# Latent attention on one core: probabilities turned by VectorE in 32x32 blocks, a batch's values summed in eight array tiles, exponentials of both heads ahead of the query copy

## What is computed

```python
q = (x @ W_q).reshape(B, S, N_HEADS, D_HEAD).transpose(0, 2, 1, 3)
latent = x @ W_kv_down
kv = (latent @ W_kv_up).reshape(B, S, N_HEADS, D_HEAD).transpose(0, 2, 1, 3)
scores = jnp.einsum('bhqd,bhkd->bhqk', q, kv) * scale
probs = jax.nn.softmax(scores, axis=-1)
out = jnp.einsum('bhqk,bhkd->bhqd', probs, kv)
out = out.transpose(0, 2, 1, 3).reshape(B, S, N_HEADS * D_HEAD)
return out @ W_o
```

## Time and profile before

| | |
|---|---|
| median of 3 runs | 1045.13 us (1040.69 to 1045.65) |
| the profiled execution | 1047.63 us, of which its span is 1045.9 us |
| busy over the span | PE 94%, PE weight load 57%, DVE 66%, ACT 47%, POOL 27% |
| this stage in the trace | first matmul at 707.65 us, last ACT copy ends at 873.01 us: 165.36 us |
| its parts | 32 pairs to 844.48, then the 64 mix matmuls for 27.89 us |

### The profile page before, as it was taken

One profiled execution on the slowest core, in us unless ns is written; L12 is line 12 of the kernel. 1 busy time (PEld: TensorE's weight loads), 2 busy tenths in 40 slices (PEclk: granted clock), 3 DMA queues, 4 the chain that ended last, 5 costly groups with the idle time before them and its releaser, 6 DMA issues. The chain is left out here.

```text
span 1045.9 us, 13773 instructions
## 1 busy us (share of the span) xinstructions
PE 980.6 (94%) x4708; PEld 599.6 (57%) x4708; DVE 690.5 (66%) x1080; ACT 487.9 (47%) x1036; POOL 279.2 (27%) x244
## 2 busy tenths in 40 slices
PE   5999989989999999998999999988999999999997
PEld 2555554365665666644645555655667676555554
DVE  2789867279999999768345545665666614567653
ACT  3632233799887886321145455535666611111112
POOL 0000000008887888310022332103545510000000
PEclk9999999999999999999999999989999999999999
DMA  4123114040000000055044443220000001211101
GB/s 128 42 65 95 51 55 131 1 123 21 21 21 21 28 14 1 1 159 171 11 132 113 101 97 75 51 61 1 1 1 2 1 1 31 60 31 30 30 1 40
DMA packets 53952, 52.84 MB, mean 51 GB/s; under 512 B 9864, under 2 KB 48873, under 8 KB 53889
## 3 DMA queue, kind: packets, MB, share of 16 engines
q1 hardware_dynamic: 48352, 46.00, 14.9%
q0 software_dynamic: 3072, 4.20, 2.6%
q10 hardware_dynamic: 2464, 1.84, 0.6%
HBM read 44.45 MB, written 5.47 MB: 48 GB/s over the span
## 5 line engine op out<-in xcount | busy, mean ns | idle before, releaser
L1085 POOL TENSOR_TENSOR seen<-state,c_row 128x512 f32<-128x512 f32 x128 | 160.5, 1276 | 103.2 <-DVE state L1105 75.9
L1105 DVE TENSOR_TENSOR_SCAN state<-decay,banks 128x512 f32<-128x512 f32 x128 | 155.3, 1216 | 14.8 <-issue 7.3
L2470 PE MATMUL banks<-xnT,weight 128*128 128x512 f32 x256 | 115.0, 592 | 1.0 <-PEq L2197 1.0
L1043 ACT ACTIVATE weighed_x<-dx_tok,b_tok 128x512 f32<-128x512 f32 x124 | 87.7, 709 | 25.7 <-PE banks L1215 24.4
L2204 POOL TENSOR_TENSOR prob<-prob,inverse 128x512 f32<-128x512 f32 x64 | 65.2, 1039 | 113.4 <-DVE inverse L2289 113.4
L1053 ACT ACTIVATE decay<-delta_pairs,A 128x510 f32<-128x510 f32 x128 | 90.5, 707 | 6.2 <-DVE state L1105 6.2
L1215 PEld LDWEIGHTS banks<-ident,weighed_x 128*128 128x128 f32 x512 | 58.6, 140 | 59.2 <-ACT weighed_x L1043 33.3
L2511 DVE TENSOR_TENSOR inter<-gelu,banks 128x512 f32<-128x512 f32 x32 | 22.0, 687 | 96.7 <-ACT gelu L2502 96.1
L2502 ACT ACTIVATE gelu<-banks 128x512 f32<-128x512 f32 x32 | 19.1, 597 | 138.2 <-PE banks L2470 138.2
L1215 PE MATMUL banks<-ident,weighed_x 128*128 128x128 f32 x512 | 80.1, 279 | 2.3 <-DVE state L1105 2.3
L2470 PEld LDWEIGHTS banks<-xnT,weight 128*128 128x128 f32 x256 | 48.6, 190 | 49.3 <-issue 47.8
(11 more groups left out here) (382 smaller groups left out, 1781.6 us busy)
## 6 DMA issues: line engine op xcount, KB each, us to landing
prob_row<-probs_dram SPq DMA_DIRECT2D x8, 512.0 KB, 3.8
c_row<-c_dram SPq DMA_DIRECT2D x32, 128.0 KB, 3.0
slot_wide_w<-in_L_ffn_w_gate SPq DMA_DIRECT2D x16, 176.0 KB
slot_wide_w<-in_L_ffn_w_up SPq DMA_DIRECT2D x16, 176.0 KB
slot_down_w<-in_L_ffn_w_down SPq DMA_DIRECT2D x16, 176.0 KB
gate_up_w<-in_L_ffn_gate_up_w SPq DMA_DIRECT2D x8, 256.0 KB, 2.9
delta_pairs<-conv_in SPq DMA_DIRECT2D x8, 256.0 KB
w_WqT<-in_L_attn_W_q SPq DMA_DIRECT2D x1, 2048.0 KB, 10.6
```

The costliest lines, as they stand in the source:

```text
L1043: nc.scalar.activation(weighed[:, v % 2, tile, :, j, :], dx_tok[:, 4 * p + tile, :].rearrange("p (g e) -> p g e", g=groups), ACT.Identity, ...
L1085: nc.gpsimd.tensor_tensor(seen[:, u % ring, :], state[:, u % ring, :], c_row[:, v % 4, :], ALU.mult).then_inc(seen_ready, 1)
L1105: nc.vector.tensor_tensor_scan(state[:, u % ring, :], decay[:, u % ring, :, :].rearrange("p b t -> p (b t)"), banks[:, 4 + u % 2, :], 0.0, ...
L2470: last = nc.tensor.matmul(banks[:, 4 + 2 * half + j, :], weight[:, s, j, k, tile * P:(tile + 1) * P], xnT[:, k, cols[half]], start=(k == 0 ...
```

## The change

- DVE's `flip` turns `prob` by a 32x32 block transpose (128x512 f32 from SBUF to SBUF), from POOL's result directly into `probT`, which now holds all pairs of two batches. PE's transposes and DVE's copies from PSUM are gone.
- A block transpose leaves keys in 32-row pieces. So `weigh` runs once per batch: for each of eight blocks of 32 keys it issues four row tiles by two heads, 64 matmuls of 512 columns, each with 32 rows and 64 output columns. Their weights are `lat_rows`, which SP fills at the stage's start with 16 DMAs out of `lat_tok` (64 KB each). They use banks 4 to 7; bank 7 is also the queries' bank.
- The sums of a batch are copied by ACT (two banks) and DVE (two banks) into `oT`, which now lies in the place of W_o's buffer. `mix(b)` runs once per batch, five pairs into the next batch, and DVE copies its result. The result lies in `xn_tok`, no longer in `s_tok`, whose memory holds `q_weight`.
- The query runs four pairs ahead, with a ring of four. ACT does both heads' exponentials, then the query copy.

The core of the diff (`place`, `score_bank`, the semaphores' names and the callers are left out; `batch_after(u, lag)` returns the batch that ended `lag` pairs before pair u starts, if one did):

```diff
-    ahead_q, ahead_s = 3, 2
+    ahead_q, ahead_s, ring_q = 4, 2, 4
+    rows = 32
+    quarters, blocks = P // rows, SEQ // rows
+    by_scalar, by_vector = (3, 0), (1, 2)
...
+        lat_rows = m.sbuf("lat_rows3", [P, NT, P // rows, LATENT])
+        q_now = m.sbuf("q_now3", [P, ring_q, SEQ])
         shift = m.sbuf("shift3", [P, 4, 2, 2])
         total = m.sbuf("total3", [P, 2, 2, 2])
         inverse = m.sbuf("inverse3", [P, 2, 2, 2])
-        prob = m.sbuf("prob3", [P, 2, 2, 2, SEQ])
-        probT = m.sbuf("probT3", [P, 2, 2, 2, SEQ])
-        oT = m.sbuf("oT3", [P, UNITS3, N])
+        prob = m.sbuf("prob3", [P, 2, 2, 2 * SEQ])
+        probT = m.sbuf("probT3", [P, 2, 2, UNITS3, 2 * SEQ])
+        oT = w["Wo"][:, :, :].rearrange("p (s u) d -> p s u d", s=2)
...
+        def sums_of(b, a):
+
+            return oT[:, b % 2, :, :].rearrange("p u (q a j) -> p u q a j", q=2, a=quarters)[:, :, :, a, :]
+
+        def bank_of(a):
+            return banks[:, 4 + a, :].rearrange("p (u q j) -> p u q j", u=UNITS3, q=2)
+
+        def mix_bank(b):
+            return 5 if b < BATCH - 1 else 0
...
+            @block.sync
+            def _(sp):
+                for part in range(P // rows):
+                    for a in range(quarters):
+                        sp.dma_start(lat_rows[a * rows:(a + 1) * rows, :, part, :],
+                                     lat_tok[part * rows:(part + 1) * rows, :, :]).then_inc(lat_moved, DMA)
+                sp.wait_ge(lat_moved, P // rows * quarters * DMA)
...
+                    last_values = (u - ahead_q) // UNITS3 - 1
+                    if last_values >= 0:
+                        pe.wait_ge(scalar_kept, 2 * last_values + 1)
...
-                def turn(u, h):
...
-                def weigh(u):
...
+                def weigh(b):
+                    if b == 0:
+                        pe.wait_ge(lat_moved, P // rows * quarters * DMA)
+                    else:
+                        pe.wait_ge(s_ready, b)
+                    pe.wait_ge(flipped, 2 * UNITS3 * (b + 1))
+                    pe.wait_ge(q_ready, min(pairs, UNITS3 * (b + 1) + ahead_q))
+                    for n in range(blocks):
+                        for a in range(quarters):
+                            part = slice(a * rows, (a + 1) * rows)
+                            for h in range(2):
+                                last = nc.tensor.matmul(
+                                    banks[h * LATENT:(h + 1) * LATENT, 4 + a, :],
+                                    lat_rows[part, 2 * b + n // quarters, n % quarters, :],
+                                    probT[part, b % 2, h, :, :].rearrange("p u (q n j) -> p (u q) n j", q=2, n=blocks)[:, :, n, :],
+                                    start=(n == 0), stop=(n == blocks - 1), skip_group_check=True)
                     last.then_inc(summed, 1)
 
-                def mix(t):
...
+                def mix(b):
+                    pe.wait_ge(scalar_kept, 2 * b + 2)
+                    pe.wait_ge(vector_kept, 2 * b + 2)
+                    for t in range(2):
+                        for u in range(UNITS3):
+                            last = nc.tensor.matmul(banks[:, mix_bank(b), t * D:(t + 1) * D], oT[:, b % 2, u, t * P:(t + 1) * P],
+                                                    o_weight[:, u, :], start=(u == 0), stop=(u == UNITS3 - 1))
+                    last.then_inc(mixed, 1)
...
-                    if u + ahead_q < pairs:
-                        query(u + ahead_q)
-                    for h in range(2):
-                        turn(u, h)
-                    if u:
-                        weigh(u - 1)
-                weigh(pairs - 1)
+                    if batch_after(u, 0) is not None:
+                        weigh(batch_after(u, 0))
+                    else:
+                        if batch_after(u, 1) is not None:
+                            query(u + ahead_q - 1)
+                        if u + ahead_q < pairs:
+                            query(u + ahead_q)
+                    if batch_after(u, 4) is not None:
+                        mix(batch_after(u, 4))
+                weigh(BATCH - 1)
                 pe.wait_ge(exp_ready, 2 * pairs)
-                for t in range(NT):
-                    mix(t)
+                mix(BATCH - 1)
...
-                def evacuate(u, h):
...
+                def flip(u, h):
+                    b, unit = place(u)
+                    dve.wait_ge(prob_ready, 2 * u + h + 1)
+                    if b >= 2:
+                        dve.wait_ge(summed, b - 1)
+                    nc.vector.transpose(probT[:, b % 2, h, unit, :], prob[:, u % 2, h, :]).then_inc(flipped, 1)
+
+                def keep_sums(b):
+                    dve.wait_ge(summed, b + 1)
+                    if b >= 2:
+                        dve.wait_ge(mixed, b - 1)
+                    for a in by_vector:
+                        nc.vector.tensor_copy(sums_of(b, a), bank_of(a)).then_inc(vector_kept, 1)
+
+                def keep_mixed(b):
+                    dve.wait_ge(mixed, b + 1)
+                    nc.vector.tensor_copy(s_tok[:, 2 * b:2 * b + 2, :].rearrange("p t d -> p (t d)"), banks[:, mix_bank(b), :]
+                                          ).then_inc(s_ready, 1)
...
-                    if u + ahead_s < pairs:
+                    behind = batch_after(u, 1)
+                    if u + ahead_s < pairs and behind is None:
                         for h in range(2):
                             top(u + ahead_s, h)
                     for h in range(2):
-                        evacuate(u, h)
+                        flip(u, h)
+                    if behind is not None:
+                        keep_sums(behind)
+                        for h in range(2):
+                            top(u + ahead_s, h)
+                    if batch_after(u, 5) is not None:
+                        keep_mixed(batch_after(u, 5))
+                keep_sums(BATCH - 1)
+                keep_mixed(BATCH - 1)
...
-                    if u >= 2:
-                        dve.wait_ge(summed, u - 1)
-                    nc.vector.tensor_copy(probT[:, u % 2, h, :, :].rearrange("p a q -> p (a q)"), banks[:, 4 + h, :]
-                                          ).then_inc(probT_ready, 1)
+                def flip(u, h):
+                    b, unit = place(u)
+                    dve.wait_ge(prob_ready, 2 * u + h + 1)
+                    if b >= 2:
+                        dve.wait_ge(summed, b - 1)
+                    nc.vector.transpose(probT[:, b % 2, h, unit, :], prob[:, u % 2, h, :]).then_inc(flipped, 1)
+
+                def keep_sums(b):
+                    dve.wait_ge(summed, b + 1)
+                    if b >= 2:
+                        dve.wait_ge(mixed, b - 1)
+                    for a in by_vector:
+                        nc.vector.tensor_copy(sums_of(b, a), bank_of(a)).then_inc(vector_kept, 1)
+
+                def keep_mixed(b):
+                    dve.wait_ge(mixed, b + 1)
+                    nc.vector.tensor_copy(s_tok[:, 2 * b:2 * b + 2, :].rearrange("p t d -> p (t d)"), banks[:, mix_bank(b), :]
+                                          ).then_inc(s_ready, 1)
 
                 for u in range(ahead_s):
                     for h in range(2):
@@ -2301,52 +2348,61 @@
                 for u in range(pairs):
                     for h in range(2):
                         invert(u, h)
-                    if u + ahead_s < pairs:
+                    behind = batch_after(u, 1)
+                    if u + ahead_s < pairs and behind is None:
                         for h in range(2):
                             top(u + ahead_s, h)
                     for h in range(2):
-                        evacuate(u, h)
+                        flip(u, h)
+                    if behind is not None:
+                        keep_sums(behind)
+                        for h in range(2):
+                            top(u + ahead_s, h)
+                    if batch_after(u, 5) is not None:
+                        keep_mixed(batch_after(u, 5))
+                keep_sums(BATCH - 1)
+                keep_mixed(BATCH - 1)
 
             @block.scalar
             def _(act):
                 def query(u):
                     act.wait_ge(q_done, u + 1)
-                    if u >= 2:
-                        act.wait_ge(scored, 2 * (u - 1))
-                    nc.scalar.activation(q_now[:, u % 2, :], banks[:, 7, 0:SEQ], ACT.Identity, scale=scale).then_inc(q_ready, 1)
+                    if u >= ring_q:
+                        act.wait_ge(scored, 2 * (u - ring_q + 1))
+                    nc.scalar.activation(q_now[:, u % ring_q, :], banks[:, 7, 0:SEQ], ACT.Identity, scale=scale
+                                         ).then_inc(q_ready, 1)
...
-                        act.wait_ge(turned, 2 * (u - 2) + h + 1)
+                        act.wait_ge(flipped, 2 * (u - 2) + h + 1)
...
-                for u in range(2):
+                def keep_sums(b):
```

(79 more changed lines are left out.)

18 lines of the change are left out of this document (6 added, 12 removed).

## The result

Over 19 runs of each kernel the changed one takes 1038.68 us in the median against 1044.42: 5.7 us less, a ratio of 0.9938 with a 95% interval of 0.9924 to 0.9952. So it is faster, inside the range and by less than the forecast's 10.0. The profiled execution took 1034.3 us (span 1032.5), the lowest of the 19, as the one of before was near its highest; whole spans of two traces can't be compared here, so I compare the stage.

The account below looks back on a forecast made before the run. PE was taken to bound the kernel at 4.01 us a pair. Afterwards, first weigh at 34.5, last at 138.3 after three batches, plus a 16.4 tail: stage 154.7 us, 10.0 less, giving 1035.1 us; range 1029 to 1051.

Parts of the forecast that it names:

- tiles run eight at once: PE's new weigh: its 64 calls of 512 columns run eight at a time, 7.0 us a weigh.
- tiles that overlap in part: Rival on weigh: tiles overlap but not fully, 10.0 us a weigh, 1047.1 us in all; chance 0.12.
- only four at a time: Rival on weigh: rows or columns go together but not both, 14 us a weigh, 1063 us; chance 0.07.
- A loop of DVE and POOL: Per pair: reciprocals, POOL's two products, second transpose in turn; 0.24 + 2.04 + 0.09 + 0.60 = 2.97 us.
- Half rate: Rival on DVE's f32 block transpose: 1.13 us each, stage 15.1 us longer, 1050.2 us; chance 0.12.
- the two getting in each other's way: Rival: DVE's first transpose waits for POOL's second product, 7.8 us in all, 1042.9 us; chance 0.05.
- A batch, 34.92: DVE's eight loops, 23.76 us, plus 3.79 for the sums, 1.61 third pair, 5.16 mix, 0.60 mixed copy.
- mix in front of a score: Once a batch, mix's 6.97 us on PE delays a score: DVE waits 5.58 us, 5.16 net.
- is worth nothing there: ACT finishing both heads before the query copy frees a score 0.28 us earlier; nothing in DVE and POOL's loop waits for it.
- Ramp and tail: Stage ends: first reciprocal at 9.1 us, first weigh at 34.5; after the last weigh's start 16.4 us, uncovered.
- clock rival: PE's clock falls as it idles: at half clock score and query add 38 us, 1073 us; chance 0.03.
- The walk of the old program: Same durations stepped through the kernel before: stage 164.7 us against 165.36 traced, so the difference, 10.0 us, was forecast.

Follow-up runs that it names:

- e5: Changed kernel with the weigh's four row tiles one after the other, so neighbouring matmuls share a row tile: 1194.75 us, weighs of 42.7 to 44.8 us.
- e11: Changed kernel with POOL multiplying only the first 128 of each row of 256 probabilities: stage 154.51 us, reciprocals 2.6 us apart in the mean.
- e4: Changed kernel with each batch's mix cut into four pieces of four matmuls, spread over later pairs: 1028.07 us, ratio 0.9817 to the kernel before.
- e3: Changed kernel with ACT's query copy put back between the two heads' exponentials: 1056.85 us, ratio 1.0097 to the kernel before.
- e2: Changed kernel with 18 dummy matmuls in PE's idle time ahead of the last weigh: 1037.96 us, last weigh 7.13 us.
- e9: Changed kernel with mix in four pieces and 8 dummy matmuls ahead of the last weigh: 1024.84 us against 1045.83 for the kernel before, ratio 0.9793.

## Why the prediction was right, and where its size was off

- *PE was the bound, its turn and small weigh are gone, tiles run eight at once.* Right: 7.13 us a weigh against 7.0 forecast. The rivals of tiles that overlap in part or only four at a time are out (7.13 and e5).
- *A loop of DVE and POOL bounds the pairs.* Right, and shown by e11: 2.91 against 2.97. Its terms: 0.20 and 0.03 for the hand-overs (0.24 and 0.09 forecast), 2.04, and 0.64 to 0.65 for a transpose (0.60). Half rate is out; 1041 ns for POOL's product beside transposes, against 1039, leaves nothing for the two getting in each other's way. Eight loops come to 23.3 where the sum has 23.76.
- *A batch, 34.92.* Measured 35.23 twice. Waits of 1.50 and 5.83 us where 1.39 and 5.58 stood. The hit is closer than its terms: against loops that were 0.5 shorter stand 0.2 more at the copies of the sums (739.56 to 746.45 less a loop, 3.98 against 3.79), 0.2 more for the third pair (746.45 to 751.20, 1.84 against 1.61) and 0.3 more at mix and the copy of its result (757.03 to 766.04, 6.10 against 5.76). That mix in front of a score makes DVE wait over 5 us was right twice (5.83); the third time it was 4.97. e4 shows the place, and that four pieces win back about half of it.
- *ACT's new order "is worth nothing there".* Wrong. The step asked what the earlier score gives in the loop of DVE and POOL, not which loop would close if the order were the old one. It is worth 18.3 us (e3), more than the whole gain; the forecast of the sum did not suffer, since the sum was made with the order in place.
- *Ramp and tail.* Here the size went, by the clock, which the sum put at nothing at both ends. The tail's weigh was put at 7.1; after 9.05 us of idling it took 8.53 and 9.13. The forecast's clock rival had even excepted "the wait at each end", and gave it no price: 1.4 to 2.0 us (e2). The first weigh was put at 34.5 and came at 35.7: the first two queries were 4.01 apart in place of 2.64, which is 1.4, so that without it the ramp is as forecast, 34.4 (an estimate). In e9, whose start was at full clock, the first reciprocal comes at 9.23 (9.1 forecast) and the low stretch behind it makes the rest. The three batches were 1.0 short.
- The range (1029 to 1051) held the time. In the first trace of after the stage, to its last copy, is 158.5 us against 154.7: 1.2 of ramp, 1.0 of batches, 1.4 of last weigh and 0.1 to 0.2 of the rest. The walk of the old program was 0.7 short as well, so the difference of the stages misses by 3.2: 6.8 in place of 10.0. Part of this is luck of the traces: the one of before had its start at full clock. The other 1.1 of the 4.3 us by which the median is off lies within the interval of the ratio (5.0 to 7.9 us).
- *A side price.* At half clock score and query were to add 38 us; by its own terms, 32 pairs of 4.06 in place of 2.97, it is 35. Nothing hangs on it.
- *Where the expected gain of a leaner PE went:* PE gave up 4.01 - 2.03 = 1.98 us a pair, 63 us in all, and got 28 of weigh back. Of the 35 left, the loop of DVE and POOL and the pieces in front of scores took most: 32 pairs at 2.91 where PE alone needs 2.03 are 28. e4 and e9 recover 9 and 12, of which 0.5 in e9 is its earlier first weigh.

## What to carry to other kernels

When the bounding engine is relieved, ask of each in-order engine not only what it does but whose result each of its waits closes into a loop: an order that is free beside a busy engine can cost 18 us once that engine waits. Long pieces of work on an engine with slack should be cut and spread: 7 us in one piece made DVE wait 5.8 us, four pieces of 1.7 made it wait 3.4 in all, since each is still longer than the slack of 0.9 a pair; pieces of that size were not tried. And price the first matmuls behind a wait of several us at the lower clock: it was low behind 4.10, 7.38 and 9.05 us, and behind 2.2 in some traces.

## What was not expected of the hardware

- PE busy for 43 of 43 us, with 32-row, 64-column tiles that run few at a time, was granted 0.50 to 0.53 of its clock (e5); the same 64 matmuls in eight tiles at a time were granted 1.00 (e2, 849.30 to 856.43). Being busy did not suffice; what made the difference no run here shows.
- Behind 4.10 us of idling came a slow weigh (8.66 us at 0.82, e4), and with 3.6 us of dummy matmuls in the same gap a full one (7.13 at 1.00, e9). The length of the idling did not order them: 7.38 us gave 9.63 at 0.73 (e11), 9.05 gave 8.53 at 0.83.
- A block transpose of 128x512 f32 took 0.70 us and 0.64 from start to start, hardly more than a copy of that size (0.69, have two in 1.29), and POOL beside it kept its pace.
